# A six-layer decoder block on one core: the first scan's decay factors and scores, the norm before the first routing, and the tails of the second scan

## The reference, cut to what matters

```python
x = ln(x + ssm0(x))            # a1, a2, a3: 24 heads, 64 states, scan over 256 steps
x = ln(x + long_conv(ctx, x))  # b1, and the norm
x = ln(x + moe0(x))            # c1 routing, c2 experts, c3 gather and mix
x = ln(x + ssm1(x))            # d1, d2: 1024 channels, 16 states, scan over 256 steps
x = ln(x + linear_attention(x, ctx))   # e
x = ln(x + moe1(x))            # f
...
# ssm0, one step, per batch and head
diff = (1 - a_t) * B_t * mean(x_t)
boost = relu(tanh(beta * mean(diff ** 2) / (ema + 1e-6)))
alpha = clip(base + (1 - base) * boost, 0.01, 0.999)
h = alpha * h + (1 - alpha) * B_t x_t;  y = C_t . h     # B_t, C_t are L2-normalised
...
# moe0 routing: softmax over 64 experts, top 8, position in the expert's queue by a cumulative count,
# tokens past position 128 are dropped; the token's row goes to slot expert * 128 + position
...
# ssm1, one step, per channel and state
h = exp(dt * A) * h + dt * B_t * u_t;  y = sum over states of C_t * h
```

## Time and profile before

| | |
|---|---|
| median of 3 runs | 5667.89 us (5663.9 to 5668.9) |
| the profiled execution: own time, span | 5655.14 us, 5653.5 us |
| TensorE's granted clock, mean | 0.873 of full speed |
| busy: PE, DVE, ACT, POOL | 75%, 50%, 28%, 25% |
| first scan, a2 | about 438 to 1884 us |
| long convolution b1, norm b2, routing c1 | about 2135 to 2360, 2372 to 2430, 2438 to 2674 us |
| second scan, d2 | about 3653 to 4612 us |

### The profile page before, as it was taken

One profiled execution on the slowest core, in us unless ns is written; L12 is line 12 of the kernel. 1 busy time (PEld: TensorE's weight loads), 2 busy tenths in 40 slices (PEclk: granted clock), 3 DMA queues, 4 the chain that ended last, 5 costly groups with the idle time before them and its releaser, 6 DMA issues. The chain is left out here.

```text
span 5653.5 us, 63809 instructions
## 1 busy us (share of the span) xinstructions
PE 4245.5 (75%) x19934; PEld 3238.9 (57%) x19934; DVE 2851.4 (50%) x5042; ACT 1596.8 (28%) x3236; POOL 1416.1 (25%) x1215
## 2 busy tenths in 40 slices
PE   7896999989999796621994068677776758864994
PEld 6784787877878444421452057555555546643773
DVE  6662333343333336732223644488887865542335
ACT  4332212122121110010221145555554532211342
POOL 0002000000000005545003700088887840002002
PEclk9997999989999898855997589888888889986997
DMA  4227111121111333342995463465334321123334
GB/s 136 99 85 279 45 48 45 48 75 48 46 47 35 135 150 108 97 171 74 341 315 177 130 132 101 155 106 86 76 71 89 71 68 52 50 86 94 101 105 120
DMA packets 437048, 607.13 MB, mean 107 GB/s; under 512 B 66390, under 2 KB 315030, under 8 KB 432288
## 3 DMA queue, kind: packets, MB, share of 16 engines
q1 hardware_dynamic: 377376, 477.94, 28.8%
q0 software_dynamic: 46464, 114.81, 6.6%
q10 hardware_dynamic: 13056, 12.59, 0.6%
HBM read 428.17 MB, written 218.92 MB: 114 GB/s over the span
## 5 line engine op out<-in xcount | busy, mean ns | idle before, releaser
L2038 PE MATMUL d_py<-d_h,d_ident 128*128 128x256 f32 x2048 | 533.4, 420 | 205.1 <-POOL d_h L1917 191.8
L1921 POOL TENSOR_TENSOR d_dBu<-d_B,d_dtu 128x1024 f32<-128x1024 f32 x256 | 597.3, 2367 | 34.8 <-DMA d_dtu<-dtu 33.6
L2038 PEld LDWEIGHTS d_py<-d_h,d_ident 128*128 128x128 f32 x2048 | 424.7, 212 | 313.8 <-POOL d_h L1917 226.8
L684 PE MATMUL a_pB<-a_uhi,a_whi 128*128 128x512 f32 x1152 | 491.4, 427 | 41.9 <-DVE a_ulo L579 41.9
L684 PE MATMUL a_pB<-a_uhi,a_wlo 128*128 128x512 f32 x1152 | 463.5, 402 | 0.0
L684 PE MATMUL a_pB<-a_ulo,a_whi 128*128 128x512 f32 x1152 | 460.8, 400 | 0.0
L1945 ACT ACTIVATE d_ph<-d_dt,d_A 128x255 f32<-128x255 f32 x1024 | 425.6, 460 | 0.0
L1988 DVE TENSOR_TENSOR_SCAN d_ph<-d_ph,d_dBu 128x1024 f32<-128x1024 f32 x160 | 365.7, 2286 | 13.9 <-POOL d_dBu L1921 13.6
L655 DVE SCALAR_TENSOR_TENSOR a_W<-a_pG,a_cB,a_M 128x256 f32<-128x256 f32 (+1 forms) x384 | 142.6, 413 | 450.9 <-PE a_pG L712 403.4
L985 POOL TENSOR_TENSOR b_kv<-b_c 128x128 f32 (+11 forms) x256 | 100.4, 435 | 959.7 <-DMA b_c<-ctx_turned 955.2
L684 PEld LDWEIGHTS a_pB<-a_uhi,a_whi 128*128 128x128 f32 x1152 | 224.4, 195 | 84.3 <-issue 31.1
(11 more groups left out here) (462 smaller groups left out, 9800.0 us busy)
## 6 DMA issues: line engine op xcount, KB each, us to landing
c_gu<-w_gu SPq DMA_DIRECT2D x64, 768.0 KB, 4.6
a_wraw<-w_bc SPq DMA_DIRECT2D x24, 1536.0 KB
slots<-a_zeros POOLq DMA_DIRECT2D x32, 512.0 KB, 12.8
c_wd<-w_down SPq DMA_DIRECT2D x64, 256.0 KB, 5.1
c_xb<-slots SPq DMA_DIRECT2D x64, 256.0 KB, 5.8
slots_y<-c_y POOLq DMA_DIRECT2D x64, 256.0 KB
f_w1r<-w SPq DMA_DIRECT2D x64, 256.0 KB, 2.8
f_w2r<-w SPq DMA_DIRECT2D x64, 256.0 KB, 2.9
```

Source lines behind the costliest of these rows:

```text
L684: ins = nc.tensor.matmul(out, a[:, k, cols], b[:, k, ts], start=(k == 0 and n == 0), stop=(k == F - 1 and n == 2))
L1921: pool.tensor_tensor(dBu[c % RB][:, :, :], B_sb[i][:, q * G:(q + 1) * G, :], dtu_sb[i][:, f, :].unsqueeze(1).to_broadcast([P, G, L]), ALU. ...
L2038: ins = nc.tensor.matmul(py[f % 2][:, 0:L], ident_sb[:, :], h_sb[c % RH][:, n, :], start=False, stop=(q == Q - 1 and n == G - 1))
```

## The change: what it does

1. **First scan, factors.** `decays` is gone, and with it `pa`. alpha of a unit (128 x 16) is stored by SP to DRAM, turned so that each sequence's alphas lie in a row (`alpha_rows`, 16 x 128), and, when that has landed, loaded back repeated into every partition (`al_all`, 8 KB each, 1 MB). SP does this (`spread`) behind the weights' load and ahead of the store of y. VectorE scans M out of `al_all`.
2. **First scan, norms.** The part of B (root, alpha, `cB`) of unit n+1 is worked out in the middle of unit n; the part of C stays at the unit's start. `half_start` is moved ahead, into the step that opens a half: on ScalarE in front of the evacuation of the first projections, on VectorE in front of the first alphas.
3. **First scan, scores.** `scores(b)` makes both heads of a sequence side by side, one on rows 0 to 63 and one on 64 to 127, with four banks `pG`: four calls a unit in place of eight.
4. **First scan, clears.** 80 pieces of 256 KB in place of 40 of 512 KB.
5. **Norm and routing** are one stage (`norm_route`) that reads b1's result in SBUF: no `r_feat`, no `x2_feat`, no loads. Per group of two tiles VectorE makes the norm of group g+1 and then the routing of g. Buffers of the scatters are four.
6. **Second scan.** A batch's tail is spread over the next one's chunks: project at chunks 0 and 2, `channel_out` at 1, moments at 5, root at 6, scaling and turning at 7 (into the banks `po`), copying at 11. POOL's last two products with C go to the next batch's first chunks, too.

```diff
-                pe.wait_ge(s_al, cur + 1)
                 pe.wait_ge(s_ut, cur * 16 + 16)
-                decays(0)
-                decays(1)
                 scores(0)
                 for i in range(NI + 1):
                     for j in slots[i]:
                         project(j)
                     if i < NI:
-                        if i + 1 < NI:
-                            scores(i + 1)
+                        if i % 2 == 0 and i // 2 + 1 < NBH:
+                            scores(i // 2 + 1)
                         output(i)
-                        if i % 2 == 1 and i // 2 + 2 < NBH:
-                            decays(i // 2 + 2)
...
+            def spread(nxt, into):
+                sp.wait_ge(s_al, nxt + 1)
+                alone(sp, tick_sp)
+                sp.dma_start(alpha_rows[into].rearrange("r t -> t r"), al[:, :, :].rearrange("p h c -> p (h c)"),
+                             allow_slow_non_contiguous=True).then_inc(s_stored, 16)
+                sp.wait_ge(s_stored, nxt * 16 + 16)
+                alone(sp, tick_sp)
+                sp.dma_start(al_all[into][:, :, :], alpha_rows[into].rearrange("(h c) t -> h (c t)", h=2).partition_broadcast(P)).then_inc(s_all, 16)
...
                         weights(0 if last else pair + 1, nxt + 1, 1 - into)
+                    if not first:
+                        spread(nxt, into)
...
-                    act.wait_ge(s_G, cur * NI)
+                    act.wait_ge(s_G, cur * NBH)
...
+                    if n == BLK - 1:
+                        act.wait_ge(s_pn, nxt * NQ + BLK)
+                        nc.scalar.activation(nB[:, :, :].rearrange("p h c -> p (h c)"), pn[:, 0:2 * TT], ACT.Sqrt).then_inc(s_rootB, 1)
+                        act.wait_ge(s_arg, nxt + 1)
+                        nc.scalar.activation(q0[:, :, :], q0[:, :, :], ACT.Tanh).then_inc(s_tanh, 1)
...
+                dve.wait_ge(s_all, cur * 16 + 16)
                 if nxt is not None:
                     weights_lo(nxt * 2 + 2, C_COLS)
...
+                    if i == ALPHA_AT and nxt is not None and not first:
+                        alphas(nxt, nxt - half * PAIRS, into)
...
-            sp.wait_ge(s_sum, HEADS + 1)
-            sp.dma_start(r_feat.rearrange("k p t -> p k t"), x_sb[:, :, :]).then_inc(s_out, 16)
-            sp.wait_ge(s_out, 16)
...
+            norm(0)
+            dve.wait_ge(s_const, 16 * CONSTS)
+            for g in range(GROUPS):
+                if g + 1 < GROUPS:
+                    norm(g + 1)
+                route(g)
...
+    GATE_AT, LAST_AT, MOMENTS_AT, ROOT_AT, SCALE_AT, TURN_AT, COPY_AT = 1, 2, 5, 6, 7, 7, 11
...
+                    if not first(b):
+                        if c == GATE_AT:
+                            channel_out(before, F1 - 1)
+                        if c == MOMENTS_AT:
+                            moments(before)
+                        if c == SCALE_AT:
+                            scaled(before)
```

More of the change, by code:

```diff
@@ L1225, in _ @@
+            root(0)
+            features(0)
+            for g in range(GROUPS):
+                if g + 1 < GROUPS:
+                    root(g + 1)
                 act.wait_ge(s_neg, g + 1)
@@ L1850, in feat, with reached, weighed, first @@
             return a[:, :, bass.ds(b * L, L)].rearrange("k p t -> p k t")
-        def later(b, done, per, back):
-            return b * per + max(done - back, 0)
+        def reached(b, done, per, back):
+            return b * per + (max(done - back, 0) if isinstance(b, int) and b == 0 else done - back)
+        def weighed(b, c, pooled, per):
+            return b * per + (weighted_before(c, pooled) if c >= 0 else -sum(on_pool(k) == pooled for k in range(C + c, C)) if not first(b) else 0)
+        def first(b):
+            return isinstance(b, int) and b == 0
+        def pipelined(eng, batch):
+            batch(0, 0, 0)
+            with eng.Fori(0, NB // 2 - 1) as r:
+                for i in range(2):
+                    batch(2 * r + 1 + i, r + i, 1 - i)
+            batch(NB - 1, NB // 2 - 1, 1)
         @block.sync
@@ L1890, in _, with batch @@
             spread(1, 1)
+            def batch(b, k, i, last=False):
+                sp.wait_ge(s_yz, b * F1)
+                alone(sp, tick_sp)
+                gates(b)
+                if not last:
+                    sp.wait_ge(s_py, b * C)
+                    alone(sp, tick_sp)
+                    streams(b + 1, 1 - i)
+                    spread(b + 1, 1 - i)
+                stores(b - 1)
+                sp.wait_ge(s_T, b * 2)
+                alone(sp, tick_sp)
+                sp.wait_ge(s_out, b * 48)
+                alone(sp, tick_sp)
+                residual(b)
@@ L1929, in _ @@
+            pipelined(pool, batch)
+            for c in range(C - LAG, C):
+                if on_pool(c):
+                    weigh(NB - 1, c, 1)
         @block.scalar
@@ new lines, in batch @@
+            def batch(b, k, i):
+                act.wait_ge(s_dt[i], k * 32 + 32)
+                before = 0 if first(b) else b - 1
+                for c in range(C):
+                    f, q = c // Q, c % Q
+                    act.wait_ge(s_scan, reached(b, c, C, 1))
+                    act.wait_ge(s_hv, weighed(b, c - 1, False, KEPT))
+                    nc.scalar.copy(ph[c % 2][:, :, 0:1], zero[:, :, :])
+                    for n in range(G):
+                        ins = nc.scalar.activation(ph[c % 2][:, n, 1:L], dt_sb[i][:, f, 1:L], ACT.Exp, scale=A_sb[:, f, q * G + n:q * G + n + 1])
+                    ins.then_inc(s_dA, 1)
+                    if not first(b) and c == ROOT_AT:
+                        root(before)
+                    if not first(b) and c == COPY_AT:
+                        turned(before)
@@ L1954, in _ @@
+            pipelined(act, batch)
+            root(NB - 1)
+            turned(NB - 1)
         @block.vector
@@ new lines, in project, with turn @@
+            def project(b, g):
+                pe.wait_ge(s_yz, b * F1 + g + 1)
+                if g == 0 and not first(b):
+                    pe.wait_ge(s_oc, b * 2)
+                for c in range(2):
+                    ins = nc.tensor.matmul(po[c][:, :], yz[:, g, c * P:(c + 1) * P], wo_sb[:, g, :], start=(g == 0), stop=(g == F1 - 1))
+                    if g == F1 - 1:
+                        ins.then_inc(s_o, 1)
+            def turn(b):
+                for c in range(2):
+                    pe.wait_ge(s_ln, b * 2 + c + 1)
+                    for k in range(KD):
+                        ins = nc.tensor.transpose(po[c][:, k * P:(k + 1) * P], x_sb[:, c, k * P:(k + 1) * P], ident_sb[:, :])
+                    ins.then_inc(s_T, 1)
```

717 lines of the change are left out of this document (332 added, 385 removed).

## The result

| | before | changed |
|---|---|---|
| median | 5665.9 us (4 runs, 5659.65 to 5668.9) | 5339.47 us (4 runs, 5336.76 to 5342.63) |
| span of the profiled execution | 5653.5 us | 5339.5 us |
| TensorE's granted clock, mean | 0.873 | 0.880 |

The ratio is 0.9425, with a 95% interval of 0.9409 to 0.9442. The forecast was 5350 (5290 to 5425), so the total was right. Its parts were not: laid stage by stage beside the trace of before, one gave more than forecast and two gave less.

What follows compares the result with a forecast made beforehand. PE was taken to bound the first scan, POOL's scatters most of routing, DVE the second scan's chunks. −120 − 115 − 80 = −315 us gave 5340 profiled, about 5353 in runs, stated as 5350 (8 in 10: 5290 to 5425).

Steps and rivals of the forecast that it cites:

- Decays removed: First scan: dropping 32 decay matmuls a unit saves 3.6 us of PE time per unit.
- Scores: First scan: four paired calls replacing eight save 2.5 us a unit, between 1.2 (taking turns) and 3.8 (wholly together).
- Opening units: First scan, unit 0: +10 us for half_start ahead of the evacuation, +8 for alphas through spread; unit 11 given nothing.
- Late spread: Rival, first scan: alphas' store and reload late by about 5 us in each of 22 units, +110 us, 5460; chance 0.14.
- slower than before: Rival, first scan: 4-byte stores plus repeated load take 42 us or more, using up the other gains; chance 0.03.
- Norm and routing: Fused stage: start earlier, four buffers remove the 14.3 us waits, POOL stays the bound; −115 us.
- bound by DVE at 24 us a group: Rival, fused norm and routing: DVE's group takes 24 us and binds the stage, +27 us, 5377; chance 0.12.
- Second scan: Tails spread over the next batch's chunks: period from 116.9 to about 105.5 us, −11.4 × 7 batches = −80 us.
- rival of a weak second scan: Second scan gives half as POOL and DVE wait for each other: period 111, +40 us, 5390; chance 0.12.
- The sum: Whole kernel: −120 first scan, −115 norm and routing, −80 second scan, together −315 us.
- The forecast's own range: Whole kernel: 5305 to 5385 us, with scores anywhere between the two ends; chance 0.59.

## Why the forecast came out, point by point

**Decays removed: right.** With eight single calls again, the unit is 3.7 us shorter than before; the forecast had 3.6.

**Scores: the term was mis-sized.** −2.5 was taken, between −1.2 and −3.8, because no row had two halves of the array at work. The measured value is the upper bound, −3.8: the paired call lasts as long as a single one. The rule of the Trainium skill that was weighed against it, "TensorE: Matmul & The Clock Gate", Part 3, The mechanism, that matmuls in different row groups overlap, agrees with this trace (starts 7 ns apart, 0.95 us for both heads). The pitch became 49.2 and not 50.2: with 3.6 + 3.8 = 7.4 us, the 22 units of the forecast, with unit 0 and without unit 11, would give 22 × 1.3 = 29 us more than forecast. Unit 12 gave only 5.7 of its 7.4.

**Opening units: too high.** +18 us had been put on unit 0. The stall did grow, by 7.7 us, in place of 10. The alphas' first trip (store issued at 527.4, load at 540.4) cost nothing, since PE had projections to do; how near that was to its limit the 37 us of the doubled store show. With its own saving, unit 0 came out at 146.7 us to its first store of y in both kernels. Units 11 and 12 and the last gave 1.9, 5.7 and 6.5 us. In sum: 20 × 7.36 + 1.9 + 5.7 + 6.5 = 161.3 of the 161.8 us.

**Late spread, and slower than before: did not occur.** 17 us in sum, as estimated; slack 7.5 us and not 10. The sign named for it, a wait of DVE for `al_all`, did show (4.6 us in four of nine units) with nothing late, so it was a poor sign. One more store of 11 us adds 82 us to this stage, but in another way than the rival has it: 1.5 us in each of 20 steady units, 30 in all, and 52 at the two units that open a half. The full price per microsecond in every unit was too high, and the opening units, which the rival leaves out, are the tighter place.

**Norm and routing: the step "with four buffers the waits of 14.3 us go; POOL stays the bound" failed.** The prediction had named gaps between the scatters as a sign of being wrong, and there they are. The start was even better (30.5 us after b1's end, 34.2 forecast), and DVE's group, 16.5 us, was a little under the 17 to 19. What was missing is that PE's completions reach VectorE up to 28 us late while POOL issues indirect DMAs without a break: 31 us of gaps. This was in the trace of before, and read wrongly (timelines of PE and of DVE, kernel before):

```profile
2493.56 3.67 PE L1295 MATMUL c_pL<-c_rw,c_xf 128*128 128x64 f32 x16 [21.62 <-DMA c_xt<-x_tok]
2506.00 0.29 DVE L1246 TENSOR_REDUCE c_mx<-c_pL 128x2 f32<-128x128 f32 x1 [29.70 <-DMA b_v<-r_feat]
```

The logits of the group were done by 2497.2, and L1246 began at 2506.0; the 14.3 us in the earlier trace rows were taken to be buffers alone, and 9 of them were this. Of the difference of 32 us to the forecast, 30 are the three gaps beyond the usual 0.3 us, 3 smaller gaps, 3 the way from the last scatter to the experts, less 4 at the start. Without the stream the stage takes the 194 us of the forecast. That the stream is the cause is shown; by what way it delays PE's semaphores is open, and so are how long a stream may be and whether its issue or its packets do it.

**The rival "bound by DVE at 24 us a group" (+27 us)** gave nearly the right size by a wrong mechanism, which is luck: DVE is busy for 103 of the stage's 227 us.

**Second scan: three errors of size in one term.** The period of before is 118.3 on average, and the row used was the shorter of an alternation (7 × 1.4 = 10 us to the good). With a tail, the period after is 108.4, not 105.5; 2 us of that are the blocked scaling, of which the sum in PSUM gives back 1.6. And the count was of periods where it should have been of batches: the first batch carries no tail, and the last carries two, the one before and its own, 124.3 us against 115.1. So −75.3 + 9.2 = −66 in place of −80. The rival of a weak second scan (period 111, +40) did not occur, though single periods with a tail alternate between 106.9 and 110.7, past the 109 that the prediction gave as a limit.

On the blocked scaling, "SBUF — State Buffer" of the Trainium skill, Who interferes with whom, states that VectorE and GpSimd share a pair of ports under an exclusive lock, that a VectorE operation with two SBUF inputs contends there with a GpSimd one that reads SBUF, as does one in a two-port mode (which a tensor_scalar can enter), and that the one that issues first holds the pair while the other blocks fully. This trace agrees: 2.32 us for a 128x2 operation with two SBUF inputs and 0.16 for the same one with GpSimd idle, 0.15 for one with a single input, 0.81 for the full scaling out of PSUM, and the scans, whose first input is in PSUM, stay at 2.3 us beside POOL's products. The prediction moved that operation next to POOL's work at its undisturbed price.

**The sum** of the changes, −315, came out at −314, because 42 us more from the first scan, and 3 from code that the change doesn't touch, met 32 and 14 us less from the other two: that is luck. The 10 us between 5350 and the median come from elsewhere: the prediction set its figure near 5353, 12.8 us over the sum, since the median of before lay that much over its profiled execution, and the changed kernel's median is 1.7 us under its own. The forecast's own range held each of these alone, but the agreement of the total says less than it seems to.

## What to carry to other kernels

Before pricing a removed wait, ask what else ends at the same moment: find when the releaser's own inputs were ready, since here 9 of 14 us belonged to a late semaphore and came back in the new kernel. When VectorE work is moved beside GpSimd arithmetic, give it one input in PSUM or expect it to wait for GpSimd's instruction as well (2 us a time here); and break up a long stream of indirect DMAs when other engines wait for TensorE meanwhile. Average a period over all its repeats, and count which repeats carry the moved work.

## What the runs showed of the hardware that was not expected

- With POOL issuing indirect DMAs 1.28 us apart, semaphores of PE were recorded up to 28 us late; fills of about the same length do not do this, nor do the rows' bytes (dropping the rows changes nothing), and a pause of 2 us or a wait of 2 to 4 us for landing after every 16 scatters ends most of it: stalls of VectorE of 4.4 to 5.8 us at most are left.
- Two 64-row matmuls in the two halves of the array take the time of one (0.95 us a call either way), in either order of issue.
- Beside a GpSimd product of 2.33 us, a VectorE operation of 128x2 with both inputs in SBUF takes 2.32 us, and 0.16 with GpSimd idle; a scaling of 128x512 takes 2.6 us, 0.54 with GpSimd idle, and 0.81 beside it with its input in PSUM.
- A store of 8 KB as 2048 runs of 4 bytes takes 11.2 us from its issue to that of the load waiting for it, though it moves less than the 48 KB that took 4.7 us in the earlier trace rows; 8 KB repeated into 128 partitions, 1 MB, lands 5.9 us after its issue.
